# First six stores of y issued between the loads of x, and the row means of the last three chunks of x taken by ScalarE

## The reference

```
edge_index = stack([src, dst])
x = x + gnn(layernorm(x), W1, b1, W2, b2, edge_index)
x = x + ffn(layernorm(x)[None], Wg, bg, W1, b1, W2, b2)[0]

gnn:  agg = segment_sum(x[nbr], dst);  cnt = segment_sum(1, dst)
      mean = agg / max(cnt, 1)
      x @ W1.T + b1 + mean @ W2.T + b2
ffn:  gates, top 2 of 8, softmax;  sum over the two of p * (relu(x W1e + b1e) W2e + b2e)
```

## Time and profile before

| what | value |
| --- | --- |
| time, median of 3 runs | 2143.47 us (2138.97 to 2146.81) |
| the profiled execution | 2127.52 us, span 2125.7 us |
| mean granted TensorE clock in it | 0.919 |
| busy: TensorE, VectorE, ScalarE, GpSimd | 85%, 48%, 41%, 58% |
| last landing of the first stage, `ytab` complete | before 115.6 us |
| first gather | 117.31 us |

### The profile page before, as it was taken

The page is one execution under the profiler, slowest core; times in us unless marked ns, Lnnn a source line. Parts: engine busy times, 40 slices in busy tenths (PEclk is TensorE's granted clock), DMA queues, the critical chain, the costliest instruction groups (busy, mean ns, idle before and its releaser), DMA issues.

```text
span 2125.7 us, 39848 instructions
## 1 busy us (share of the span) xinstructions
PE 1805.4 (85%) x10626; PEld 1521.5 (72%) x10626; DVE 1013.3 (48%) x2245; ACT 863.8 (41%) x2483; POOL 1224.3 (58%) x1147
## 2 busy tenths in 40 slices
PE   4868888789877598776777589999999999999997
PEld 3745665577645476555556467899999999999997
DVE  6848866787757685543444356631111111111111
ACT  3721651156411264411111167654444444444443
POOL 1156667677776677766667653344544544544443
PEclk9979999999988798888898786999999999999999
DMA  9223223323333323334444365762344242442421
GB/s 298 83 82 92 75 86 91 88 84 88 90 92 92 88 84 90 87 91 123 119 120 122 91 199 185 245 207 58 98 119 117 37 118 36 119 119 36 117 39 16
DMA packets 113326, 224.32 MB, mean 106 GB/s; under 512 B 27479, under 2 KB 76797, under 8 KB 107319
## 3 DMA queue, kind: packets, MB, share of 16 engines
q0 software_dynamic: 61376, 129.59, 24.3%
q1 hardware_dynamic: 31568, 74.06, 10.3%
q10 hardware_dynamic: 20262, 19.24, 2.9%
HBM read 374.14 MB, written 35.04 MB: 192 GB/s over the span
## 4 chain that ended last, share of the span: by engine, by line
PE 69%; issue 9%; DVE 8%; another core or an unknown queue 5%; POOL 2%; SPq 2%; ACT 2%; DMA 1%; DVEq 1%; ACTq 0%; POOLq 0%
PE bank L1185 21%; PE bank L1220 18%; PE bank L1236 17%; PE bank L977 5%; POOL arena L607 2%; DVE agg L1837 2%; PE bank L1061 1%; PE bank L1208 1%; PE bank L1023 1%; SPq L457 1%; ACT arena L736 1%; DVE arena L1342 1%; DVE arena L1547 1%; PE bank L1095 1%
## 5 line engine op out<-in xcount | busy, mean ns | idle before, releaser
L607 POOL DMA_INDIRECT arena<-ytab,arena x784 | 827.5, 1055 | 355.7 <-issue 214.9
L1185 PE MATMUL bank<-arena 128*128 x2356 | 671.9, 425 | 136.1 <-ACT arena L736 56.5
L1185 PEld LDWEIGHTS bank<-arena 128*128 128x128 f32 x2356 | 468.4, 211 | 244.3 <-issue 180.7
L870 ACT ACTIVATE arena<-bank,agg 128x128 f32<-128x128 f32 x848 | 311.0, 368 | 410.3 <-PE bank L1220 335.8
L736 ACT ACTIVATE arena<-arena 128x1024 f32<-128x1024 f16 x148 | 156.3, 1056 | 671.3 <-DVE arena L1547 462.6
L1837 DVE TENSOR_TENSOR agg<-agg,bank 128x257 f32 x589 | 247.3, 420 | 374.8 <-PE bank L1185 157.4
L1220 PEld LDWEIGHTS bank<-arena,agg 128*128 128x128 f32 x3392 | 396.2, 192 | 5.2 <-ACT arena L870 0.2
L1220 PE MATMUL bank<-arena,agg 128*128 128x128 f32 x3392 | 397.9, 276 | 0.0
L1236 PE MATMUL bank<-agg,arena 128*128 128x256 f32 x1696 | 383.8, 379 | 1.3 <-DMA agg<-in_b 1.3
L640 POOL DMA_INDIRECT out<-arena x106 | 172.6, 1629 | 327.5 <-issue 246.4
L1236 PEld LDWEIGHTS bank<-agg,arena 128*128 128x128 f32 x1696 | 314.0, 190 | 40.1 <-DMA agg<-in_b 1.8
(11 more groups left out here) (263 smaller groups left out, 1514.3 us busy)
## 6 DMA issues: line engine op xcount, KB each, us to landing
agg<-in_w SPq DMA_DIRECT2D x212, 1024.0 KB
agg<-in_b SPq DMA_DIRECT2D x106, 128.0 KB
arena<-ytab,arena POOLq DMA_INDIRECT x784
ytab<-arena SPq DMA_DIRECT2D x12, 512.0 KB, 2.9
arena<-in_xt ACTq DMA_DIRECT2D x24, 256.0 KB
node<-in_x SPq DMA_DIRECT2D x6, 896.0 KB, 12.4
agg<-in_xt SPq DMA_DIRECT2D x6, 896.0 KB, 13.1
out<-node ACTq DMA_DIRECT2D x6, 896.0 KB
```

The lines of the kernel that those rows point to most:

```text
L607: pool.indirect_dma_start(out=rows[:, v % RU, h, 0:D], out_offset=None, in_=ytab[:, :], in_offset=bass.IndirectOffsetOnAxis(ap=rowidx[g % ...
L870: act.activation(hT[:, m, :], hidden_bank(j, m)[:, 0:T], ACT.Relu, bias=b1b[:, b, m:m + 1]).then_inc(s_fr, 1)
L1185: mm = pe.matmul(bank[bank_of(n)][:, 0:W], onehot[n // QUAD % 2][:, n % QUAD, h, :], pair[:, h * W:(h + 1) * W], start=(h == 0), stop=(h = ...
```

## The change

The loads of `src` and `dst` get a semaphore each, and VectorE's first step waits for `src` alone. Store 0 is issued behind the loads of chunk 4, store 1 behind those of chunk 5, store 2 behind those of chunk 6 and the last rows, store 3 behind `gw1t`, store 4 behind the two biases, store 5 behind the gates' weights; the others follow as before. Each is still preceded by its wait for `s_y`. The sums and means of chunks 4, 5 and 6 leave VectorE and GpSimd: ScalarE takes each block's negative mean by a copy of the row, scaled by -1/256, with an accumulated sum, in `spread(t)` for block t+2, ahead of the squares of t. That makes 21 such instructions; the number of squares, roots and copies of y stays the same. GpSimd then waits for four sums only before it clears `agg`.

```diff
+BY_DVE = 4
-        junk = [onehot[k // 8][:, k % 8 // 2, k % 2].bitcast(F16) for k in range(U)]
+        junk = [onehot[k // 8][:, k % 8 // 2, k % 2].bitcast(F16) for k in range(2 * U)]
...
-            sp.dma_start(src_i[0:EP, :], src.rearrange("(p c) -> p c", p=EP)).then_inc(s_edge, 16)
-            sp.dma_start(dst_i[0:EP, :], dst.rearrange("(p c) -> p c", p=EP)).then_inc(s_edge, 16)
+            sp.dma_start(src_i[0:EP, :], src.rearrange("(p c) -> p c", p=EP)).then_inc(s_src, 16)
+            sp.dma_start(dst_i[0:EP, :], dst.rearrange("(p c) -> p c", p=EP)).then_inc(s_dst, 16)
+
+            def store_y(j):
+
+                n = min(4, NT - 4 * j)
+                sp.wait_ge(s_y, 4 * j + n)
+                b = j % 3
+                sp.dma_start(y_v[:, 4 * j:4 * j + n, :], ybuf[:, 4 * b:4 * b + n, :]).then_inc(s_yst[b], 16)
+
             for i in range(NB):
...
-            sp.dma_start(node[0:TAIL, NT - 1, :], x[(NT - 1) * P:N, :]).then_inc(s_x[NB - 1], 16)
+                if i == NB - 1:
+                    sp.dma_start(node[0:TAIL, NT - 1, :], x[(NT - 1) * P:N, :]).then_inc(s_x[NB - 1], 16)
+                if i >= NB - 3:
+                    store_y(i - NB + 3)
             sp.dma_start(gw[:, 0], gw1t.rearrange("(k p) n -> p k n", p=P)).then_inc(s_w, 16)
+            store_y(3)
...
+            store_y(4)
...
+            store_y(5)
...
-            for j in range(-(-NT // 4)):
-                n = min(4, NT - 4 * j)
-                sp.wait_ge(s_y, 4 * j + n)
-                b = j % 3
-                sp.dma_start(y_v[:, 4 * j:4 * j + n, :], ybuf[:, 4 * b:4 * b + n, :]).then_inc(s_yst[b], 16)
+            for j in range(6, -(-NT // 4)):
+                store_y(j)
...
-            for i in range(NB):
+            for i in range(BY_DVE):
                 means(i)
...
+            def mean(t):
+
+                if t % U == 0:
+                    act.wait_ge(s_x[t // U], 16 if t // U < NB - 1 else 32)
+                act.activation(junk[U + t % U], row_of(t), ACT.Copy, scale=-1.0 / D, accum_out=less_mean[:, t:t + 1]).then_inc(s_lma, 1)
+
             def squares(t):
 
-                if t % U == 0:
+                if t >= BY_DVE * U:
+                    act.wait_ge(s_lma, t + 1 - BY_DVE * U)
+                elif t % U == 0:
                     act.wait_ge(s_lm, t // U + 1)
...
             def spread(t):
 
+                if BY_DVE * U <= t + 2 < NT:
+                    mean(t + 2)
                 squares(t)
...
-            v.wait_ge(s_edge, 32)
+            v.wait_ge(s_src, 16)
...
+            v.wait_ge(s_dst, 16)
             step(v.tensor_scalar(s_, d_, 7, 7, ALU.bitwise_and, ALU.logical_shift_left))
...
-                if t in (1, 3, 5):
-                    sums(4 + (1, 3, 5).index(t))
```

More of the change, by code:

```diff
@@ L369, in gnn_moe @@
         G = range(NG)
-        s_const, s_tail0, s_clear, s_edge, s_w, s_w2t = (sem(n) for n in (
-            "consts", "tail_zeroed", "sums_cleared", "edges_in", "weights_in", "w2t_in"))
+        s_const, s_tail0, s_clear, s_src, s_dst, s_w, s_w2t = (sem(n) for n in (
+            "consts", "tail_zeroed", "sums_cleared", "src_in", "dst_in", "weights_in", "w2t_in"))
         s_x = [sem(f"x_in{i}") for i in range(NB)]
-        s_sumx, s_lm, s_sqx, s_std, s_rstd = (sem(n) for n in ("summed", "less_mean", "squared", "std", "rstd"))
+        s_sumx, s_lm, s_lma, s_sqx, s_std, s_rstd = (sem(n) for n in ("summed", "less_mean", "less_mean_by_act", "squared", "std", "rstd"))
         s_w2s, s_w2c = sem("w2_summed"), sem("w2_centred")
```

## The result

| | before | changed |
| --- | --- | --- |
| time, median of 5 runs each | 2144.34 us | 2133.35 us (2129.47 to 2135.25) |
| ratio, 95% interval | | 0.9951 (0.9936 to 0.9966) |
| first gather (GpSimd) | 117.31 us | 108.99 us |
| first placed tile (VectorE) | 77.37 us | 69.05 us |

A forecast was written before the change was run, and what follows sets the result against it. VectorE's list, stalled 8.9 us through ScalarE's wait for store 0, was taken as the bound. Stall, echo and 5.8 of sums, about 15, less some 5 for means, left 9.5: 2143.5 - 9.5 = 2134.0 us, range 2127 to 2143.

The forecast's parts named there:

- VectorE's list, not `ytab`, ends the first stage: First gather at 117.31 us starts 1.6 us after VectorE released it; the last store of y landed before 115.6.
- The wait for store 0: ScalarE's 11.1 us wait before copy 12 and VectorE's 8.9 us wait for TensorE are one wait seen twice.
- The head: VectorE's first step waiting for `src` alone gains 0: it meets a gate at 17.94 us, the centring of W2.
- SyncE's standing: SyncE stands 4.5 us at store 0, until 32.35 us; DMA work still queued, so it costs nothing.
- The landings: Stores 0 to 3 land at about 39.0, 45.2, 51.7 and near 54 us, just in time for ScalarE's copies.
- ScalarE becomes the pace-maker: Turns t = 16 to 36 with a mean of 0.49 us take 1.34 instead of 0.85; VectorE's ranks follow ScalarE.
- `reciprocals(2)` at 44.1: Without `sums(4)`, VectorE starts rank slot 2 at about 41.4 us and reaches this reciprocal 2.6 us later.
- The sum: Roots 5 end at 67.5 us, first tile 67.8, 9.6 earlier; 0.1 lost in placing; first gather 107.8.
- One to one to the end: A shift of the first gather carries fully to the end; distance from gather to end stays 2008.4 us.
- Rival 1: Stores land with the loads' lag, copy 12 at 45 us, copy 20 at 57; ScalarE loses 5: 2139; chance 0.14.
- Rivals 2, 3 and 5: Mean 0.69: 2137, chance 0.09; ScalarE bounding placing, with table loads 2161, 0.06; mean 0.36: 2131.5, within the forecast's 0.62.
- Rival 4: First gather is earlier, but the gathering stage ends as before, having waits of its own: 2143; chance 0.09.

The follow-up runs named there:

- stores_only: Changed kernel with all sums and means back on VectorE and GpSimd, only the stores between the loads; ratio to the kernel before 0.9968.
- means_only: Changed kernel with all stores of y behind the loads as before, means of the last three chunks on ScalarE; ratio to before 1.0003.
- head_only: Kernel before with the head part alone: VectorE's first step waits for src instead of src and dst; ratio to before 0.9998.
- late_head: Changed kernel, but VectorE waits for src and dst at its first step, as before the change; ratio to before 0.9961.
- late_both: Changed kernel with VectorE waiting for src and dst at the start and the first clearing of agg after block 14; ratio to before 0.9961.
- by_dve5: Changed kernel with the means of chunk 4 left to VectorE and GpSimd, only chunks 5 and 6 on ScalarE; ratio to before 0.9933.
- mean_twice: Changed kernel with each mean on ScalarE taken twice, the extra copy into unused room; ratio to before 0.9994.
- late_clear: Changed kernel, but GpSimd clears the first chunk of agg only after block 14 of y instead of block 7; ratio to before 0.9970.
- after_again: The changed kernel without an edit, profiled and timed again beside the experiments; ratio to before 0.9963.
- before_again: The kernel before without an edit, a second profile and timing; ratio to before 1.0001.

## Why the prediction was right, point by point

- **VectorE's list, not `ytab`, ends the first stage.** That held. The 1.59 us in the first gather's row are not time after VectorE's release, as the prediction reads them, but idle time that this release ends.
- **The wait for store 0 is what the kernel pays for.** Shown: `stores_only` brings 6.8 of 8.2 us, `means_only` 0.3.
- **The head is worth 0.** Shown by `head_only` and by the 5.19 us that VectorE stands in the changed kernel.
- **SyncE's standing costs nothing.** Not quite. The DMA engines had work, but not enough for all of them. Two windows around SyncE's standing, first of the kernel before, then of the changed one; the last three figures are TensorE's granted clock, DMA share and GB/s:

```profile
31.50:33.50 2.00, 1.00 1.04 371
33.50:36.00 2.50, 1.00 1.08 377
```

```profile
31.50:33.50 2.00, 0.50 0.77 284
33.50:36.00 2.50, 0.66 1.03 313
```

  The shortfall is 87 x 2.0 + 64 x 2.5 = 334 KB, at 374 GB/s 0.9 us.
- **The landings.** In the changed kernel stores 0 and 1 landed within 0.3 us of the sum. Store 2 was mis-sized: 53.6 instead of 51.7, of which the 0.9 us above is one part; the rest was not taken apart. "Just in time" was thus the tightest step, and store 2 is the bound as soon as ScalarE gets to it faster: `late_head`, `late_both`, `by_dve5`.
- **ScalarE becomes the pace-maker, 1.34 us a turn.** The mechanism is shown by `mean_twice` and `by_dve5`; the turn was 1.24, since a mean takes 0.40 and not the square's 0.49. From copy 14 to the end of roots 5 that made 22.0 us (46.87 to 68.83) where 23.4 had been summed.
- **`reciprocals(2)` at 44.1.** The step that failed: 46.55. TensorE's 28 matmuls up to the first rank part took 9.12 us at the low clock instead of 6.67, and VectorE needs that rank part. TensorE's timeline before, then changed:

```profile
29.51 6.67 PE L1023 MATMUL bank<-gw,agg 128*128 128x256 f32 x28 [3.37 <-ACT arena L701]
```

```profile
29.48 9.12 PE L1043 MATMUL bank<-gw,agg 128*128 128x256 f32 x28 [3.34 <-ACT arena L719]
```

  On VectorE the 2.7 us read as 1.36 us more in line 1536, beside GpSimd's memset, and then 0.93 and 0.42 us of waits for TensorE. But the first of these is time in which VectorE would have waited anyway. From the start of `sums(3)` to `reciprocals(2)`:

  | kernels | 28 matmuls | L1536 | to reciprocals(2) |
  | --- | --- | --- | --- |
  | before, less `sums(4)` (11.10 - 1.93) | 6.67 | 0.58 | 9.17 |
  | `late_head` | 6.67 | 1.94 | 10.53 |
  | `late_clear`, `late_both` | 8.00 | 0.58 | 10.81 |
  | `means_only`, `mean_twice` | 8.00 | 1.94 | 10.81 |
  | changed | 9.12 | 1.94 | 11.92 |
  | `after_again` | 9.37 | 1.94 | 12.18 |

  At the full clock the memset costs its 1.36 us. At the low clock it costs nothing up to here (10.81 with it and without it), and the rest follows the matmuls: 1.12 us more of them, 1.11 us later. The two rows behind the middle of the table:

```profile
45.16 0.20 DVE L1499 RECIPROCAL rstd<-std 128x7 f32<-128x7 f32 x1
```

```profile
45.12 0.20 DVE L1494 RECIPROCAL rstd<-std 128x7 f32<-128x7 f32 x1
```

  They are of `late_clear` (`sums(3)` at 34.35) and of `means_only` (34.31). So the term that the sum left out is TensorE's clock. "Which then clears `agg` earlier, under other work" was booked at nothing too; its cover had a hole, and the clock hid it here. Behind this step store 2 was next in line at 53.6, so neither could have given back more than 0.7 us.
- **The sum.** First tile 69.05 instead of 67.8, first gather 108.99 instead of 107.8: 8.3 of the 9.5 us. That is two errors against each other, 2.4 us too early for `reciprocals(2)` and 1.4 us too much for the means. The 0.1 us booked for the placing was not lost. That the time, 2133.35 us, lies within 0.7 us of the forecast is therefore in part luck: the first stage gave 8.3 us, and the median of the kernel before came out at 2144.34 with two more runs instead of 2143.47.
- **One to one to the end.** It held within some 3 us, no closer: 7.6 us timed for 8.05 in `after_again`, 6.5 for 6.9 in `stores_only`, but 6.3 for 9.1 in `late_clear` and 12.3 for 10.1 in `by_dve5`. The sign that the prediction named, a distance from first gather to end that grew, was there in the first profile (2023.4 for 2008.4) and not in the second (1897.0, against 1902.1 in `before_again`).
- **The rivals.** Rival 1 fell as it stood (landing 6.4 to 8.0 us after issue for the first two), but store 2 came with 11.2 us, close to the loads' 13. Rivals 2, 3 and 5 on the mean's price: it was lower than forecast, without a table load, and this did not buy what 5 promised. Rival 4 fell: the interval of the ratio leaves out 1 both times that the changed kernel was timed.

## What to carry to other kernels

Where a ring of buffers drains through the same queue as a block of loads, look for the engine that stands on the first full ring, and interleave the drains so that each is issued when its data is ready; moving arithmetic off a waiting engine first gains next to nothing (0.3 us here, 1.2 to 1.5 once the wait was gone). A wait put on the issuing queue must leave enough work in it for all DMA engines. And a step that is freed to run earlier, even one "off the path", should be checked against what now runs beside it. Where two delays end at the same wait, only the later one costs: read it from kernels that have one of them, not by adding up the rows.

## What the runs showed of the hardware that I had not expected

**A memset of GpSimd stops a VectorE instruction.** In the changed kernel L1535 starts at 37.12, the memset at 37.24 lasts 1.98 us (1.59 elsewhere) and ends at 39.22, and L1536, begun at 37.72, ends at 39.66, 0.44 us behind it. The small memset behind it, 0.11 us elsewhere, then takes 0.53 and ends at 39.70, right behind L1536:

```profile
39.17 0.53 POOL L598 MEMSET agg<- 128x7 f32 x1
```

That the memset is the cause is shown by `late_clear`, which only moves it: 0.58 again. L1536 has one SBUF input. Line 1362, with one input from PSUM and one from SBUF, ran at its usual 0.57 us at 52.96, beside the memset of 52.57 to 54.16. The Trainium skill, page "SBUF — State Buffer", section "SBUF: two separate sides", says that VectorE and GpSimd share a pair of ports, as an exclusive lock held for the whole of an instruction by whoever starts first, when the VectorE instruction is in a two-port mode. The trace agrees in both directions: the memset waits for L1535, and L1536 for the memset. That L1536 runs in such a mode no row shows.

**TensorE's clock around a short gap.** With a gap of 3.1 to 3.4 us without matmuls the granted clock stayed 1.00 in four profiles (both of before, `head_only`, `late_head`) and fell, at times between 28.4 and 31.4 us, in ten, in some before the gap was over and in others up to 1.2 us behind it. While low it was 0.50, the lower of the two levels (1.2 of 2.4 GHz), and the 28 matmuls behind the gap took 7.71 to 9.37 us instead of 6.67. What decides it was not found.

**A copy with an accumulated sum is cheaper than a square with one.** 0.40 against 0.49 us in steps, on the same tile and output type. They differ in more than the function, since the square also has a per-partition bias and the copy's scale is a constant; no run separates the two.
